# Cross-attention values of a Perceiver layer: one matmul per head against one matmul per pair of heads

## The reference

```
x = x + cross_attention(layernorm(x), ctx, ctx)     # 16 heads of 64, causal mask
x = x + self_attention(layernorm(x))                # 16 heads of 16, causal mask
x = x + ffn(layernorm(x))                           # 704 wide, 4-bit block quantised, silu gate
```

## Time and profile before

| what | value |
|---|---|
| median of 3 runs | 584.04 us (582.31 to 585.48) |
| the profiled execution's own time | 583.32 us |
| its span in the profile | 581.4 us |
| granted TensorE clock, mean over the span | 0.976 of full speed |
| stage one (cross-attention) | from the start to about 305 us |
| one pass of the PE loop in the steady part | 17.25 us |

### The profile page before, as it was taken

One profiled execution on the slowest core, in us unless ns is written; L12 is line 12 of the kernel. 1 busy time (PEld: TensorE's weight loads), 2 busy tenths in 40 slices (PEclk: granted clock), 3 DMA queues, 4 the chain that ended last, 5 costly groups with the idle time before them and its releaser, 6 DMA issues.

```text
span 581.4 us, 18921 instructions
## 1 busy us (share of the span) xinstructions
PE 536.8 (92%) x7928; PEld 428.8 (74%) x7944; DVE 445.5 (77%) x867; ACT 234.0 (40%) x477; POOL 44.9 (8%) x83
## 2 busy tenths in 40 slices
PE   4979999999999999999985789999999999999865
PEld 3769888889888888888764667777777777777543
DVE  3728789888889888888850569888888888888852
ACT  1323233323233323332343556555555555555211
POOL 5000100000000000000020111111111111111100
PEclk9989999999999999999987989999999999999987
DMA  8991221112211012222200000000000000000000
GB/s 256 347 280 74 72 72 28 45 72 72 72 72 55 18 72 72 72 72 74 75 3 3 3 3 2 9 9 9 9 9 9 9 9 9 9 9 10 10 9 19
DMA packets 13801, 31.03 MB, mean 53 GB/s; under 512 B 976, under 2 KB 10704, under 8 KB 11728
## 3 DMA queue, kind: packets, MB, share of 16 engines
q1 hardware_dynamic: 13776, 30.67, 15.8%
HBM read 28.57 MB, written 2.10 MB: 53 GB/s over the span
## 4 chain that ended last, share of the span: by engine, by line
PE 49%; issue 29%; DVE 13%; ACT 5%; POOL 3%; POOLq 0%; DVEq 0%; ACTq 0%
PE bank L375 10%; PE bank L397 10%; PE bank L422 9%; PE bank L366 9%; PE bank L413 4%; ACT x_oT L504 2%; DVE f_xn L1398 2%; POOL f_rstd L1091 2%; DVE f_h L1407 1%; PE bank L1182 1%; DVE f_amax_x L1493 1%; DVE f_xn L1532 1%; PE bank L1204 1%; ACT a_kblocks L1306 1%; PE bank L1158 1%
## 5 line engine op out<-in xcount | busy, mean ns | idle before, releaser
L375 PEld LDWEIGHTS bank<-x_xcT,xwk 128*128 128x128 f32 x512 | 61.9, 198 | 2.8 <-issue 1.1
L375 PE MATMUL bank<-x_xcT,xwk 128*128 128x128 f32 x512 | 62.3, 282 | 1.4 <-ACT x_xcT L487 1.4
L397 PE MATMUL bank<-xwv,x_xcT 128*128 128x512 f32 x128 | 59.7, 609 | 1.0
L422 PE MATMUL bank<-xwo,x_oT 128*128 128x256 f32 x256 | 59.7, 388 | 0.8 <-ACT x_oT L504 0.8
L366 PE MATMUL bank<-x_xcT,xwq 128*128 128x128 f32 x512 | 59.8, 275 | 0.0
L366 PEld LDWEIGHTS bank<-x_xcT,xwq 128*128 128x128 f32 x512 | 58.5, 192 | 0.0
L422 PEld LDWEIGHTS bank<-xwo,x_oT 128*128 128x128 f32 x256 | 48.6, 195 | 7.7 <-issue 1.4
L518 ACT COPY x_k_blocks<-bank 64x512 f32<-64x512 f32 x32 | 18.6, 581 | 87.8 <-PE bank L375 87.6
L1158 PE MATMUL bank<-wdT,f_hqT 128*128 128x256 f32 x192 | 47.5, 399 | 4.2 <-DVEq L1423 2.3
L1306 ACT ACTIVATE a_kblocks<-bank,head_rows 128x256 f32<-128x256 f32 x128 | 48.4, 499 | 0.0
L1182 PE MATMUL bank<-wgT,f_xqT 128*128 128x192 f32 (+1 forms) x128 | 42.2, 474 | 3.6 <-DVE f_out L1364 3.6
(11 more groups left out here) (152 smaller groups left out, 938.6 us busy)
## 6 DMA issues: line engine op xcount, KB each, us to landing
x_ctx_slab<-in_ctx_dram SPq DMA_DIRECT2D x16, 1028.0 KB, 4.8
out_dram<-f_out SPq DMA_DIRECT2D x16, 128.0 KB, 1.7
xall<-in_x_dram SPq DMA_DIRECT2D x1, 1280.0 KB, 16.2
x_first_keys<-in_ctx_dram SPq DMA_DIRECT2D x4, 320.0 KB, 12.2
xwk<-in_L_xattn_w_k_dram SPq DMA_DIRECT2D x1, 1024.0 KB, 5.1
xwq<-in_L_xattn_w_q_dram SPq DMA_DIRECT2D x1, 1024.0 KB, 7.1
xwv<-in_L_xattn_w_v_dram SPq DMA_DIRECT2D x1, 1024.0 KB, 10.3
xwo<-in_L_xattn_w_o_dram SPq DMA_DIRECT2D x1, 1024.0 KB, 12.8
```

The source lines that it names most:

```text
L375: last = nc.tensor.matmul(bank[2 + j // 4][:, (j % 4) * P:(j % 4 + 1) * P], xwk[:, k, j * P:(j + 1) * P], xcT[:, KD + k, :], start=(k == 0 ...
L397: last = nc.tensor.matmul(bank45[:, half, :], xcT[:, KD + k, :], xwv[:, k, half * 512:(half + 1) * 512], start=(k == 0), stop=(k == KD - 1))
L422: last = nc.tensor.matmul(bank67[:, 0, 0:D], oT[:, j].rearrange("p b q -> p (b q)"), xwo[:, j, :], start=(j == 0), stop=(j == XP - 1))
```

## The change

Three things change. `weigh` takes two heads at a time: the weights are 32 rows x 128 columns of v (both heads of a pair), the moving operand the 32x64 probabilities of both, and the result has 128 partitions x 64 columns, of which the two blocks that cross the heads are not used. There are 32 matmuls for a tile in place of 64, and each of the banks 2 to 5 is filled over all its 512 columns. `copy_o` becomes four copies of 64 partitions x 512 elements: first banks 4 and 5 (two copies, for the even and the odd heads), which raise the new semaphore `s_ob`, then banks 2 and 3 (two copies), which raise `s_oc`. `project_v` waits for `s_ob` in place of `s_oc`; `output` still waits for `s_oc`. And in PE's loop `turn(t+2)` moves from behind `project_v(t+1)` to between `weigh(t, t+1)` and `scores(t+1)`.

```diff
-                s_o, s_oc = sem("out_ready"), sem("oT_ready")
+                s_o, s_ob, s_oc = sem("out_ready"), sem("oT_banks_4_5_ready"), sem("oT_ready")
...
                     def project_v(t, last_o):
                         if last_o is not None:
-                            pe.wait_ge(s_oc, last_o)
+                            pe.wait_ge(s_ob, last_o)
...
-                        for h in range(H):
-                            j, half = h // 2, (h % 2) * XD
+
+                        for j in range(XP):
                             for b in range(BT):
                                 rows = slice(b * SQ, (b + 1) * SQ)
-                                last = nc.tensor.matmul(bank2345[half:half + XD, b, j * SQ:(j + 1) * SQ],
-                                                        v[rows, h * XD:(h + 1) * XD], pT[rows, h, :],
-                                                        start=True, stop=True, tile_position=(b * SQ, half))
+                                last = nc.tensor.matmul(bank2345[:, b, j * 2 * SQ:(j + 1) * 2 * SQ],
+                                                        v[rows, j * P:(j + 1) * P],
+                                                        pT[rows, 2 * j:2 * j + 2, :].rearrange("p h q -> p (h q)"),
+                                                        start=True, stop=True, tile_position=(b * SQ, 0))
                         last.then_inc(s_o, 1)
...
                         project_k(t + 1)
                         project_q(t + 1)
                         weigh(t, t + 1)
+                        turn(t + 2)
                         scores(t + 1)
                         project_v(t + 1, t + 1)
-                        turn(t + 2)
                         output(t)
...
                     def copy_o(t):
                         act.wait_ge(s_o, t + 1)
-                        nc.scalar.copy(oT[:].rearrange("p j b q -> p b j q"),
-                                       bank2345[:, :, 0:XP * SQ].rearrange("p b (j q) -> p b j q", q=SQ))\
-                            .then_inc(s_oc, 1)
+                        for at, done in ((BT // 2, s_ob), (0, s_oc)):
+                            for i in range(2):
+                                rows = slice(i * XD, (i + 1) * XD)
+                                last = nc.scalar.copy(
+                                    oT[rows, :, at:at + BT // 2, :].rearrange("p j b q -> p b j q"),
+                                    bank2345[rows, at:at + BT // 2, :].rearrange(
+                                        "p b (j i q) -> p b j i q", i=2, q=SQ)[:, :, :, i, :])
+                            last.then_inc(done, 1)
```

## The result

The changed kernel takes 590.12 us (median of 4 runs, 589.65 to 591.88) against 584.75 us for the kernel before in the runs beside it: a ratio of 1.0105, 95% interval 1.0066 to 1.0143. It is slower by about 1%. The prediction was 589.3 us, slower with a chance of 0.63.

What follows compares the result with a forecast made beforehand. PE's start-to-start times were taken to bound stage one. Passes +5.85, first pass -2.6 and last two tiles +2.0 made +5.25 us on 583.32: 588.6, with 0.72 for the median 589.3 us; the forecast's own range 586 to 595.

Steps and rivals of the forecast that it cites:

- weighing, a tile: PE's weighing to scores: 1.91 us with 64 pairs at 28.0 ns where 1.42 us stood, +0.49 us a tile.
- transposes, a tile: Transposes now between two packed groups on PE: one more change of shape, +0.10 us a tile.
- wait of the values, a tile: Scores to values on PE: the wait for ACT's copy goes, 1.17 us to 1.03 us, -0.14 us a tile.
- thirteen passes: Steady passes of tiles 1 to 13, at +0.45 us each: +5.85 us.
- first pass: PE's pause in the first weighing, read as late instructions, moves into the scores and shrinks from 3.03 to 1.2 us: -2.6 us.
- the last two tiles: End of stage one: +0.17 left of weigh(14) and the values' wait, weigh(15) +0.49, copies before last output +1.33; together +2.0 us.
- The pace of the new weighing: New weighing on PE: 128-column loads, four places at once, set 28.0 ns a pair, 1.76 us for 64 pairs.
- The two small terms: Per tile on PE: the step from the last weighing record (0.15 us) and the extra change of shape (0.10 us).
- The step out of the weighing: From the start of the last weighing record to PE's next work: 0.15 us, as in the old kernel.
- the change of shape: PE's extra switch between packed groups and the transposes' 128x128 matmuls: +0.10 us a tile.
- The copies: ACT's first pair frees banks 4 and 5 0.24 us before the values; all four add +1.33 us before the last output.
- the sum: Whole kernel: 5.85 - 2.6 + 2.0 = +5.25 us on the profiled execution's 583.32 us.

Runs made afterwards that it cites:

- m1: Changed kernel with only the even head's 32 probability columns moving through the 128-column weights of the weighing; 590.82 us in one execution.
- m3: Changed kernel with weights of 96 columns in the weighing, 64 moving columns; 583.8 us in one execution.
- m2: Changed kernel with weights of 64 columns (even heads only) in the weighing, 64 moving columns; 579.2 us in one execution.
- e1: Changed kernel with the transposes, turn(t + 2), back behind project_v; 594.14 us, ratio to the kernel before 1.0178.
- e4: Kernel before with SP's loads of the FFN and self-attention weights (3 MB) issued only after the first weighing; 579.41 us, ratio 0.9922.
- e2: Kernel before with only the transposes moved up between weighing and scores; 584.8 us, ratio 1.001.
- b2: b1 with the weighing's even and odd heads next to each other in order; 578.87 us, ratio to the kernel before 0.9894.
- e3: Kernel before with its copy cut in two by pairs of banks, values waiting for the first half only; 583.06 us, ratio 0.9984.
- b1: Kernel before with the copy cut in two and SP's later weight loads held until after the first weighing; 577.94 us, ratio 0.9875.
- m5: Changed kernel with SP's later weight loads issued only after the first weighing; 588.72 us, ratio to the kernel before 1.0089.

## Why the prediction was right

By its own steps, with the spans at marks of the chain (k products of tiles 2 and 15; the end of the stage at 305.54 and 311.19 us):

| step | predicted | measured |
|---|---|---|
| weighing, a tile | +0.49 | 1.95 - 1.42 = +0.53 |
| transposes, a tile | +0.10 | 0.58 - 0.44 = +0.14 |
| wait of the values, a tile | -0.14 | 1.03 - 1.17 = -0.14 |
| thirteen passes | +5.85 | 13 x (17.79 - 17.26) = +6.9 |
| first pass | -2.6 | 19.72 - 22.12 = -2.4 |
| the last two tiles | +2.0 | 34.11 - 32.30 = +1.8 |

- **The pace of the new weighing** decided the sign, and it came from the right row. Eight matmuls with one moving column, at 111.9 ns each, had shown that a load of 128 columns takes that long by itself; a quarter of it, 28.0 ns, stood against 27.6 measured. m1 to m3 show that the reason holds too. The Trainium skill, "TensorE: Matmul & The Clock Gate", section LDWEIGHTS (loading the stationary operand), says that a load costs by its columns whatever its rows; m1 to m3 agree for loads of 32 rows. The same page's section Part 3: Packing small matmuls — row/col tiling lets a load run beside a matmul only in other rows; m1 does not agree, since 32 moving columns fewer in the same rows changed next to nothing (27.3 ns a pair against 27.6).
- **The two small terms** a tile were a little low. The step out of the weighing was 1.95 - 1.74 = 0.21 us, not 0.15, and the change of shape 0.14, not 0.10. Over 13 passes this is the +1 us by which that row of the table is off.
- **The copies** landed as reckoned. In the pass, the pair for banks 4 and 5 ends at 161.72 + 2.37 / 2 = 162.90, 0.29 us ahead of the values at 163.19 (0.24 predicted). The measured start of the copies after the start of the last weighing record is 0.35 us, not 0.26. Of that, 0.05 us is the record itself, 270 ns long in place of 218; its weight columns and not its moving columns make it longer (271 ns in m1 with 32 moving columns, 217 in m2 with 64). PE came later by as much as the copies. At the end of the stage the output started 299.14 - 294.61 = 4.53 us after the start of the last weighing in place of 2.92, 1.61 us more where 0.49 + 1.33 = 1.82 were predicted: the sum had kept the step from the last copy to the output, which was 0.38 us before and is 0.14 now.
- **The first pass** went as its reading said: PE ran on to nearly the same place in its list and stopped there until nearly the same time. In the changed kernel 53 records of the scores were through, and PE went on at 38.33 us (before 38.59). The DMA share in the pause was 1.10 (36.97 to 38.30 us). Counted with the waits ahead of transposes (2) and scores (3), the pause stands at instruction 64 + 64 + 128 + 8 + 106 + 5 = 375 of the loop, in e1 at 64 + 64 + 128 + 116 + 3 = 375, and before at 374. With the shorter pause the clock stayed at full speed (1.00 from 38.40 to 40.40 us, where the earlier trace rows have 0.50). e4 shows that the pause hangs on the DMA load. That it is the supply of instructions is argued from this and not seen; the Trainium skill, "Runtime: NRT & Kernel Launch", section Instruction fetch mechanics, has them come in by DMA in blocks. The larger instruction queue on the page of the profile fits that, with 15 packets (0.25 MB) for 18 (0.29 MB) before, but does not say when they came.
- **What the sum left out.** The profiled executions are 590.0 - 581.4 = 8.6 us apart in span, but the stage only 311.19 - 305.54 = 5.65. The other 2.95 us lie in self-attention and FFN, which the change does not touch: PE entered them at a lower mean clock, 0.66 against 0.82 of full speed. In the changed kernel (window, us, busy PE, PEld, DVE, ACT, POOL, clock, DMA share, GB/s)

```profile
311.00:330.00 19.00, 11.75 (x74) 9.28 (x79) 2.09 (x3) 5.76 (x16) 0.00 (x0) 0.66 0.01 2
```

and in the kernel before

```profile
305.40:324.00 18.60, 11.61 (x190) 9.52 (x192) 2.78 (x5) 8.12 (x23) 0.00 (x0) 0.82 0.01 4
```

The same 16 matmuls of self-attention's second tile stand in the chains with 2.06 us before and 3.80 us in the changed kernel:

```profile
319.36 2.06 PE bank L1204 x16
326.04 3.80 PE bank L1210 x16
```

The matmuls behind them in the chain start at 324.81 before and at 333.22 in the changed kernel, so 8.41 - 5.65 = 2.76 of the 2.95 us have come together by then. That changed execution was the slowest of its four (591.88 us). By the medians, 5.4 us is the difference, and 5.25 was the sum. That they agree to 0.2 us is luck, for two reasons. The interval of the ratio allows anything from 3.9 to 8.4 us. And the sum is better than its parts deserve: +1.1 us in the passes met a start that was 0.7 us earlier (26.11 for 26.79 at the loop), which no step had. The change does not touch what lies ahead of the loop; over the profiles of all kernels here the loop starts between 26.00 and 27.28 us.

## What to carry to other kernels

Count weight columns, not matmuls, when small f32 matmuls are packed: with 64 to 128 weight columns in four places of 32 rows, a pair here cost 0.21 to 0.23 ns for each weight column, and fewer, wider matmuls made a slower whole. Look at the moving columns as well where they are many beside the weights: the scores' 14.0 ns for 32 weight and 64 moving columns is not a pace of weight columns. Before a copy is made longer to give a shorter wait, look whether the old copy can be cut in two as it stands. A pause in the middle of a run of instructions, where nothing is waited for, deserves a look at what the DMA queues carry at that time: one wait on SP's side was worth more here than the rest together.

## What the runs showed that was not expected

The pause of the first pass cost over 4 us with its half clock, and holding back 3 MB of loads removed all but 0.26 us of it. They were issued between 24 and 38 us; the FFN weights among them were first read at 71.6 us, those of self-attention behind the end of stage one. Sixty-four-column loads ran at 10.0 ns a pair in eight places and 15.0 in four, so two column halves of the same rows gave a factor of 1.5, not 2 (with the caveat above on m2's moving columns), and their order did nothing. And the clock at the end of the stage differed between kernels with the same work there: the last output took 3.72 us in e2, e4 and b2, from 5.1 to 5.4 us in the kernel before, the changed kernel, e1, e3 and b1, and 6.48 us in m5. The mean granted clock in it was 1.00 in e2 and e4, 0.68 before and in b1, and 0.56 in m5, so up to 2.8 us of an execution's time hangs on when the clock falls. It does not go with the kernel's speed (b1 took 5.41 us there and b2 3.72); what decides it stays open.
